# First batch's key and value fills in other slots of a hand-ordered Perceiver kernel

## What is computed

```python
x = x + L0_xattn(layernorm(x), ctx, ...)    # the context's mean, projected
x = x + L0_attn(layernorm(x), ...)          # self-attention, 64 tokens, 16 heads, ALiBi
x = x + L0_ffn(layernorm(x), ...)           # experts and a shared feed-forward
x = x + L1_xattn(layernorm(x), ctx, ...)    # q, k, v, softmax over 1601 keys, 16 heads of 16
x = x + L1_attn(x, ...)                     # convolution, gated recurrence, feed-forward
x = x + L1_ffn(x, ...)                      # ternary weights, 8-bit activations
```

## Time and profile before

| | us |
|---|---|
| median of 3 runs | 2113.03 |
| lowest, highest | 2110.51, 2119.26 |
| profiled execution, whole | 2115.58 |
| its span, first to last instruction | 2113.7 |
| TensorE busy | 1970.0 (93%) |
| VectorE, ScalarE, GpSimd busy | 1287.9, 1049.1, 674.4 |
| mean granted TensorE clock | 0.985 |

### The profile page before, as it was taken

One profiled execution on the slowest core, in us unless ns is written; L12 is line 12 of the kernel. 1 busy time (PEld: TensorE's weight loads), 2 busy tenths in 40 slices (PEclk: granted clock), 3 DMA queues, 4 the chain that ended last, 5 costly groups with the idle time before them and its releaser, 6 DMA issues.

```text
span 2113.7 us, 72766 instructions
## 1 busy us (share of the span) xinstructions
PE 1970.0 (93%) x31780; PEld 1585.4 (75%) x31796; DVE 1287.9 (61%) x2276; ACT 1049.1 (50%) x1532; POOL 674.4 (32%) x1349
## 2 busy tenths in 40 slices
PE   6889999999999999999999989999999998999987
PEld 4677677877877877787877877787787777777764
DVE  2556556756666567656656666565666576665644
ACT  3355445555455554555555555564545444444441
POOL 4323242423243233333323324342424222232201
PEclk7999999999999999999999999999999999999999
DMA  5533433433423343434242524334242331213122
GB/s 176 181 126 107 141 113 117 142 127 110 153 100 133 111 144 101 149 121 146 95 135 79 172 98 135 125 125 132 94 138 91 114 96 62 78 51 107 50 72 70
DMA packets 124472, 243.92 MB, mean 115 GB/s; under 512 B 13952, under 2 KB 44800, under 8 KB 124160
## 3 DMA queue, kind: packets, MB, share of 16 engines
q1 hardware_dynamic: 123568, 239.23, 34.5%
q10 hardware_dynamic: 592, 0.04, 0.0%
HBM read 235.94 MB, written 3.15 MB: 113 GB/s over the span
## 4 chain that ended last, share of the span: by engine, by line
PE 76%; DVE 8%; ACT 7%; issue 5%; POOL 2%; DMA 0%; SPq 0%; POOLq 0%; DVEq 0%; ACTq 0%
PE M L817 12%; PE M L824 11%; PE SC L1035 10%; PE SC L1058 8%; PE O L1079 8%; PE X L874 5%; ACT probT L1279 4%; PE SC L1051 3%; DVE mx L1628 3%; PE M L874 3%; PE X L1145 2%; PE M L918 1%; PE M L879 1%; PE X L853 1%; PE X L1119 1%
## 5 line engine op out<-in xcount | busy, mean ns | idle before, releaser
L1628 DVE TENSOR_REDUCE mx<-SC 128x4 f32<-128x1600 f32 (+1 forms) x256 | 466.9, 1824 | 161.0 <-PE SC L1035 157.4
L1279 ACT ACTIVATE probT<-SC 128x2048 f32<-128x2048 f32 (+1 forms) x256 | 398.7, 1557 | 160.4 <-PE SC L1058 159.9
L657 POOL TENSOR_TENSOR rowsT<-raw,rowsT 128x256 fp32r<-128x256 f32 (+1 forms) x512 | 325.8, 667 | 375.9 <-ACT rowsT L1333 375.8
L824 PE MATMUL M<-wvs,rowsT 128*128 128x256 f32 x2496 | 358.4, 292 | 3.8 <-issue 1.8
L817 PE MATMUL M<-rowsT,wks 128*128 128x400 f32 (+1 forms) x1536 | 342.3, 364 | 5.7 <-ACT kT L1220 1.6
L1220 ACT ACTIVATE kT<-M,bk 128x400 f32<-128x400 f32 (+1 forms) x256 | 151.4, 593 | 376.5 <-PE M L817 376.1
L824 PEld LDWEIGHTS M<-wvs,rowsT 128*128 128x128 f32 x2496 | 314.8, 192 | 24.2 <-issue 3.2
L817 PEld LDWEIGHTS M<-rowsT,wks 128*128 128x128 f32 x1536 | 272.4, 191 | 79.6 <-issue 63.5
L1424 DVE TENSOR_TENSOR V<-M,bv 128x512 f32<-128x512 f32 (+1 forms) x224 | 145.3, 649 | 269.5 <-PE M L824 264.2
L1035 PE MATMUL SC<-kT,bdq 32*128 32x400 f32 (+1 forms) x2048 | 245.9, 548 | 27.7 <-ACT probT L1279 23.3
L1079 PEld LDWEIGHTS O<-probT,V 128*17 128x17 f32 x13312 | 193.7, 99 | 77.0 <-issue 72.0
(11 more groups left out here) (281 smaller groups left out, 2441.4 us busy)
## 6 DMA issues: line engine op xcount, KB each, us to landing
ring<-in_ws_dram SPq DMA_DIRECT2D x428, 256.0 KB, 4.4
summed<-in_ctx_dram SPq DMA_DIRECT2D x60, 800.5 KB, 4.6
raw<-in_ctx_dram SPq DMA_DIRECT2D x64, 384.0 KB, 4.6
raw<-in_ctx_dram SPq DMA_DIRECT2D x32, 512.0 KB, 4.2
ring<-rounded_scratch SPq DMA_DIRECT2D x64, 256.0 KB, 4.0
raw<-in_ctx_dram SPq DMA_DIRECT2D x32, 321.0 KB, 4.4
out_dram<-x SPq DMA_DIRECT2D x16, 128.0 KB, 2.1
kT<-in_ctx_dram SPq DMA_DIRECT2D x2, 800.5 KB, 8.8
```

The source lines that it names most:

```text
L657: ins = pool.tensor_tensor(rowsT[1][:, c, part], raw[:, c, part], rowsT[0][:, c, part], ALU.subtract)
L824: mm = pe.matmul(bank[:, (t - 2 * a) * D:(t - 2 * a + 1) * D], rowsT[xp][:, cc, t * P:(t + 1) * P], wvs[wp][:, cc, :], start=(at == cc == ...
L1279: act.activation(probT[step % 3][0:w, :, 0:len(ts), :].rearrange("p j t q -> p j (t q)"), SC[0:w, :, 0:len(ts) * P], ACT.Exp)\
L1628: dve.tensor_reduce(mx[c][:, :, n], SC[:, :, 0:KCH[n][1]], AX.X, ALU.max).then_inc(max_used, 1)
```

## The change

The table EARLY of batch 0's fills is written anew. The key fills of slot -16 go to slot -15, ahead of that slot's own two. `value(1)` leaves slot -12; values 2 to 6 leave slots -7 to -3. Values 1, 2 and 3 now stand in slots -6, -5 and -4, where 3, 4 and 5 stood; slots -7 and -3 hold none. Values 4, 5 and 6 come from FIRST, in slots 0, 1 and 2, half "first", as for every other batch: the condition in `pieces` now lets the `OWN` fills of batch 0 through.

```diff
-EARLY = {-17: [key(0, 0), key(0, 1)], -16: [key(1, 0), key(1, 1)], -15: [key(0, 2), key(1, 2)], -12: [value(0), value(1)], -9: [key(0, 3)], -8: [key(1, 3)], -7: [value(2)], -6: [value(3)], -5: [value(4)], -4: [value(5)], -3: [value(6)]}
+EARLY = {-17: [key(0, 0), key(0, 1)], -15: [key(1, 0), key(1, 1), key(0, 2), key(1, 2)], -12: [value(0)], -9: [key(0, 3)], -8: [key(1, 3)], -6: [value(1)], -5: [value(2)], -4: [value(3)]}
...
-        if 0 < batch < B:
+        if (what in OWN or batch) and 0 <= batch < B:
             yield batch, *what
```

## The result

The changed kernel took 2107.19 us in the median of 22 runs (2097.16 to 2114.15), the kernel before 2112.11 (2106.34 to 2123.09). Their ratio is 0.9962, with a 95% interval of 0.9949 to 0.9974: 8.0 us faster (5.5 to 10.8). The two medians lie only 4.9 us apart, the means of the same runs 7.3; the size of the gain is known no better than that. The forecast was 6.4 us, 2106.6; the stated range of 2101 to 2113.5 held the median of 2107.19.

The account below looks back on a forecast made before the run. TensorE bounds the middle, so only the first 130 us's chain of waits could yield: 2.6 + 0.5 + 1.55 + 0.4 - 0.33 + 3.3 - 1.6 = 6.4 us off the median 2113.03, giving 2106.6; range 2101 to 2113.5.

Parts of the forecast that it names:

- Exponential first: Layer 0's first softmax: exponential at 38.9 instead of 41.55, gaining 2.6 us, plus 0.5 from a transpose at full clock.
- The forecast of the transpose behind the projection: Sign of being right: the transpose behind the output projection comes at about 54.1 instead of 58.79.
- Value 1: Slot -12: without its drain the normalization stands behind one value drain instead of two; 1.55 us gained, bounds 1.5 to 2.6.
- one of the prediction's own signs of being wrong: A context sum or transfer that now ends after the drain it precedes was due; no size given.
- Value 2: Slot -7, between transpose and queries' projection: 0.4 us gained, since ScalarE's context sum precedes the drain; upper bound 1.43.
- Value 6, values 1 to 3: Slot -3 emptied, and values 1 to 3 beside the maxima instead of 3 to 5: nothing gained; bound 0.7 for slot -3.
- Slot 0: Value fill placed in TensorE's wait before the maxima, beside half a key fill, overruns the wait: 0.33 us lost.
- The clock in slots 1 and 2: Values in the gaps keep TensorE at full clock for the maxima and weighing: 3.3 us gained, bounds 0 and 3.8.
- the 1.1 that was set for it: Sign of being right: waits of under 1.1 us before the maxima of slots 1 and 2, at full clock.
- The fall before the maxima: Without value 2 before the first maxima, a spell at 1.2 GHz over them: 1.6 us lost, bounds 0 and 3.2.
- rival (b): Before the first maxima the clock does not fall, giving 2105.0 us; chance 0.14.

Follow-up runs that it names:

- the dummies: Kernel before with six dummy matmuls in the gap before slot 1's maxima and four before slot 2's, no fill moved; ratio 1.0017, slots 0 to 3 in 21.90 us.
- the two other traces with empty gaps: Kernel before with only the exponential moved first (slots 0 to 3 in 24.27 us), and kernel before with ten more dummy matmuls at the start (27.18 us).
- the kernel with the dummies alone: Changed kernel plus seven dummy matmuls in TensorE's waits, four in slot -11 and three ahead of slot -9's first fill; one execution, 2112.8 us.

## Why the prediction came out

The places of the gain were right: the exponential, and the clock in slots 1 and 2. That 2106.6 lies so near the measured 2107.19 is luck in part, for the loss forecast before the maxima (1.6) didn't come, and value 1's gain (1.55) hardly arrived; these two errors largely cancel.

*Exponential first: 2.6 and 0.5.* Right. ScalarE took it at 38.43, 4.87 from the key fills' start instead of 7.51. Projection 3.0 earlier, 3.1 in the run of this part alone. The last event before the second transpose was in the first trace not GpSimd's product, though, but the bank: 43.66 stands behind the drain of the last key fill. The forecast of the transpose behind the projection, 54.1, is 20.2 from the key fills' start; it came at 18.29, 20.50 and 19.69. In the first trace the clock stayed up through the projection (1.10 instead of 2.05), which the prediction had as its upper bound, and that time was lost again in the next fill.

*Value 1: 1.55.* The drain that it takes from VectorE's queue was read rightly, the term mis-sized. I priced the removal up to the next transpose and not up to the first maxima. Two things took it back there that the trace of before had shown as harmless: the clock, which fell at another place, and, in the first trace alone, the context sum, which with its transfer is bound to the sum before it. What arrived at the first maxima is 0.84 between two first traces and 0.2 in the mean, less than one kernel's traces differ. The row for the sum stood in the trace of before: at 54.32 it had waited 3.38 for its transfer, and 2.96 us of idle time ahead of the copy were all its margin. A sum that ends after the drain it precedes was due is one of the prediction's own signs of being wrong, and it came once.

*Value 2: 0.4.* 0.54 (queries' transpose to first maxima 3.63 instead of 4.17). The drain did come right behind the context sum, at 64.48.

*Value 6, values 1 to 3: nothing.* 21.01 from the first maxima to slot 0, 21.02 before.

*Slot 0: 0.33 lost.* Nothing was lost: its maxima come 3.40 after its scores' start instead of 3.37. With the value fill ahead of it the half key fill takes 0.55 on the chain; its row there says 0.71 and overlaps its neighbour's, and the sum took 0.81 from the row of before.

*The clock in slots 1 and 2: 3.3.* Right to 0.1 with slot 0 taken in (25.13 less 21.85), and shown to be the clock by the dummies. The size holds for the trace of before that it was read from; the two other traces with empty gaps would give 2.4 and 5.3. The wait before slot 2's maxima, 1.19, is a little over the 1.1 that was set for it.

*The fall before the maxima: 1.6 lost.* It didn't come in the changed kernel; that is rival (b), to which 0.14 was given. The reasoning was that 1.5 us or less of busy time, as before 100.6, would bring the clock down; there were 1.40 in the first trace, and it held there, and fell after as much in the kernel with the dummies alone. Without it the sum is 8.0, with value 1 at 0.2 to 0.84 in place of 1.55 and no loss in slot 0 it is 7.0 to 7.6; the traces give 8.36, 8.19 and 7.08 to slot 3's maxima, and the ratio 8.0.

*The rest of the run.* The first traces differ by 10.5 and not 8.4 because the key fills began 0.4 earlier and the rest, from slot 3 on, took less. The ratio's 8.0 us can't single out one of these sums, its interval being 5.5 to 10.8. From the exponential of slot 3 to the last one it was 1940.1 before and 1937.4, 1936.1 and 1935.1 in the changed kernel, but 1933.4 to 1945.8 in the edited ones: one execution can't settle 3 us.

The Trainium skill, "TensorE: Matmul & The Clock Gate", section "What's actually happening", says that the watch on activity runs freely. By that rule the falls move from one execution to the next, and the three traces of one kernel agree: the clock fell at 53.0; at 45.4; at 48.6 and 55.4. What the Trainium skill says of transposes in Part 4 of the same page stays open: with two groups of transposes of 0.60 and 0.66 in each, and TensorE busy for 2.38 and 2.23 us of 42.0 to 45.4, the clock held in the first trace and fell in the second.

No kernel tried is clearly better than the changed one; value 1 staying in slot -12 is as good within the intervals.

## What to carry to other kernels

Price an edit up to the next point where all engines meet, not up to the next instruction: list what else ends within the time you gain, transfers that hang on a chain of their own first. When a step moves, look at what SP has queued behind its semaphore; moving one sum by two slots delayed weights that nobody had thought of, and with the clock that fell while they were awaited slot 0 came 4.1 us later (57.38 instead of 53.29). A gap that TensorE waits through is a good place for work that must be done anyway, both for the time and for the clock of what follows, and a gap left by removing work can have a price. Where the clock's falls move from one execution to the next, take more than one trace of each kernel before a term of a microsecond is called measured.

## What the runs showed of the hardware

One kernel's clock fell at different places in its three executions, with 1.3 us between the resulting first maxima (32.28 and 33.56), while slots at full clock repeated to 0.01 us. After the same 1.40 us of TensorE's busy time in 3.4 us the clock held in one kernel and fell in another. Dummy matmuls of 0.25 us each kept the clock as well as real fills did (1.47 us of them in a gap of 2.1, clock 1.00 from 92.2 to 114.1). The row of a group of three matmuls among others was 0.71 long, where the group added 0.55 to the chain.
